# Two-layer graph network with residual and layer norm: successive matmuls of an accumulation alternate between the two PSUM banks of a pair

## The chip, the cores and the metric

The kernel runs on one core of a Trainium2 chip. The metric is the device time of the program in microseconds (us). Before the change it is 2921.07 us, the median of three runs (2920.2 to 2923.01).

## The reference, cut to what matters

```python
def sage_conv(x, src, dst, W_l, b_l, W_r):        # x: 100000 x 256, 25000 edges, dst is sorted
    agg = segment_sum(x[src], dst, 100000)
    deg = segment_sum(ones, dst, 100000)
    return (agg / maximum(deg, 1)[:, None]) @ W_l + b_l + x @ W_r
h = relu(sage_conv(x, src, dst, W1_l, b1, W1_r))
h = relu(sage_conv(h, src, dst, W2_l, b2, W2_r))
out = layernorm(x + h @ W3 + b3)                  # no scale, no shift, eps 1e-5
```

All weights are 256 x 256, and everything is float32.

## The kernel before

**Precision.** Every product is made of three matmuls in fp32r. A float32 operand is split into a high part (ScalarE copies it to fp32r) and a low part (VectorE subtracts the high part from the original), and hi x hi, hi x lo and lo x hi are added up in PSUM. The contraction over 256 features takes K = 2 steps, so one accumulation of a 256 x 256 weight has 6 matmuls.

**PSUM.** There are four tensors `pair[0..3]` of 128 x 2 x 512 floats. Each is two banks: index 0 and 1 of the middle dimension. Together they are the whole PSUM.

**Two kinds of accumulation.** `columns` (line 851) has the weight block as stationary operand and 512 rows of activations as moving operand (128x512 output). Its caller loops over `m` = 0, 1: column block m goes into bank m, so all matmuls of bank 0 come first, then all of bank 1. `by_rows` (line 862) has 128 rows of activations as stationary operand and the weight as moving operand (128x256 output). Its caller loops over `s` = 0 to 3: row blocks 0 and 1 are the two halves of bank 0, blocks 2 and 3 those of bank 1, one block after the other. `turn` (line 845) transposes 128x128 blocks.

**Row stage.** 196 groups g of 512 rows pass through three layers as if there were no edges. The loop body has u = 0 to 3 (g = 4i + u), and its order is written out by hand for each engine, with semaphores between them. TensorE, in the body at line 952: transposes of group g+2 (`turn_rows`), first layer of g+1 (`columns`, 12 matmuls), an edge piece that depends on u, third layer of g-1 (`by_rows`, 24 matmuls, waits for `hlo_ok[1]`, the low part of the second layer's result), second layer of g (`columns`, 12 matmuls). The edge pieces are: u = 0 and u = 1, eight transposes of gathered rows; u = 2, 24 matmuls by rows for source rows; u = 3, 48 matmuls by rows for destination rows.

ScalarE, body at line 522: `high_x(g+2)`, a square root, `high_h` of the first layer of g+1, an edge copy, `normalise(g-2)`, `high_h` of the second layer of g. `high_h` (line 482) is the only consumer in this stage that takes the two banks one at a time:

```python
for k in range(K):
    act.wait_ge(l_ps[n], g * K + k + 1)
    nc.scalar.activation(ps[:, k], ps[:, k], ACT.Relu, ...)   # L486
act.wait_ge(hf_ok[n], (g + 1) * K)
nc.scalar.copy(h_hi[:, h], ps[:, :, :])                       # L488
```

VectorE, body at line 741: `low_x` (L643), `factors` (L698, L700), `low_h` of the first layer (L647), the edge piece (u = 0: L717 and two scans L721; u = 1: L725 and L727), the residual sum (L669, waits for both banks of the third layer), four `bn_stats` (L681), four `bn_aggr` (L692), `low_h` of the second layer (L647). VectorE takes the results of `by_rows` only when both banks are complete (L669, L731, L738).

**Edge stage.** After the rows come 49 steps j of 512 edge slots (line 1010): `turn_edges(j+1)` (16 transposes; waits for `c_mlo_ok`, the low part of the mean of step j), the second layer of j by `columns` with two weights (24 matmuls: 12 for bank 0, then 12 for bank 1), the third layer of j-1 by rows (24 matmuls). ScalarE (line 577) takes `dst_high(j+1)`, `finish_edges(j-3)` (L568), `second(j, 0)` (relu of bank 0, L553), `mean_high(j+1)` (L548), `second(j, 1)`, `second_high(j)` (L557). VectorE (line 817) takes the residual, factors, two scans (L776), `low_dst` (L787), `means` (L781), the statistics, `mean_low` (L791) and `low_second` (L795).

SyncE loads rows and stores results; GpSimd adds b3 to x (L391, waits for L669 of an earlier group) and issues the indirect DMAs. Neither waits for an accumulation of `columns`.

Of the kernel before, what the change touches and what calls it, by code (L numbers as in the profile page):

```python
# [5 lines left out]
P = 128  # L6
S = 4
# [6 lines left out]
def build(nc, x, src, dst, W1_l, b1, W1_r, W2_l, b2, W2_r, W3, b3, out):  # L14
# [12 lines left out]
    N, D = x.shape  # L27
    E = src.shape[0]
    K = D // P
# [11 lines left out]
    X1R, X2R, X3, X1L, X2L = range(5)  # L41

    with ExitStack() as ctx:
        def sb(name, shape, dt=f32):
            return ctx.enter_context(nc.sbuf_tensor(name, shape, dt))

        def pb(name):
            return ctx.enter_context(nc.psum_tensor(name, [P, K, G], f32))

        def sem(name):  # L50
            return ctx.enter_context(nc.semaphore(name))
# [11 lines left out]
        w_hi = sb("w_hi", [P, 5, K, D], f32r)  # L63
        w_lo = sb("w_lo", [P, 5, K, D], f32r)
        xn = sb("xn", [P, U, S, D])
        xb = sb("xb", [P, 2, S, D])
        xt_hi = sb("xt_hi", [P, 2, K, G], f32r)
        xt_lo = sb("xt_lo", [P, 2, K, G], f32r)
        h_full = sb("h_full", [P, 2, K, G])
        h_hi = sb("h_hi", [P, 3, K, G], f32r)  # L70
        h_lo = sb("h_lo", [P, 3, K, G], f32r)
# [3 lines left out]
        xe_hi = sb("xe_hi", [P, 2, K, G], f32r)  # L75
        xe_lo = sb("xe_lo", [P, 2, K, G], f32r)
# [3 lines left out]
        mean_hi = sb("mean_hi", [P, K, G], f32r)  # L80
        mean_lo = sb("mean_lo", [P, K, G], f32r)
# [25 lines left out]
        pair = [pb(f"pair{n}") for n in range(4)]  # L107
# [22 lines left out]
        l_ps = [sem("l1_ps"), sem("l2_ps")]  # L130
        l3_ps = sem("l3_ps")
# [7 lines left out]
        xs_ps, xd_ps, src_ps, dst_ps = sem("xs_ps"), sem("xd_ps"), sem("src_ps"), sem("dst_ps")  # L139
# [12 lines left out]
        c_hs_ps, c_hd_ps, c_l2_ps, c_l3_ps = (sem(n) for n in (  # L152
            "c_hs_ps", "c_hd_ps", "c_l2_ps", "c_l3_ps"))
# [5 lines left out]
        def after(eng, s, value):  # L159

            if not (isinstance(value, int) and value <= 0):
                eng.wait_ge(s, value)
# [681 lines left out]
        def _(pe):  # L844
            def turn(ps, rows_of, k):

                for s in range(S):
                    ins = nc.tensor.transpose(ps[:, k, s * P:(s + 1) * P], rows_of[:, s, k * P:(k + 1) * P], ident[:, :])  # L848
                return ins

            def columns(parts, ps, m):

                first = True
                for w, hi, lo in parts:
                    for k in range(K):
                        for wx, a in ((w_hi, hi), (w_lo, hi), (w_hi, lo)):
                            end = k == K - 1 and a is lo and w == parts[-1][0]
                            ins = nc.tensor.matmul(ps[:, m], wx[:, w, k, m * P:(m + 1) * P], a[:, k], start=first, stop=end)  # L858
                            first = False
                return ins  # L860

            def by_rows(parts, ps, s):

                first = True
                for w, hi, lo in parts:
                    for k in range(K):
                        for a, wx in ((hi, w_hi), (hi, w_lo), (lo, w_hi)):
                            end = k == K - 1 and a is lo and w == parts[-1][0]
                            ins = nc.tensor.matmul(ps[:, s // 2, s % 2 * D:(s % 2 + 1) * D], a[:, k, s * P:(s + 1) * P],  # L869
                                                   wx[:, w, k], start=first, stop=end)  # L870
                            first = False
                return ins

            def turn_rows(i, u, ps):
                pe.wait_ge(x_in[u], 16 * (i + 1))
# [1 line left out]
                    turn(ps, xn[:, u], k).then_inc(xt_ps, 1)  # L877

            def first_layer(b, ps):
                for m in range(K):  # L880
                    columns([(X1R, xt_hi[:, b], xt_lo[:, b])], ps, m).then_inc(l_ps[0], 1)

            def second_layer(h, ps):
                for m in range(K):
                    columns([(X2R, h_hi[:, h], h_lo[:, h])], ps, m).then_inc(l_ps[1], 1)

            def third_layer(g, ps):
                pe.wait_ge(hlo_ok[1], g + 1)
                for s in range(S):
                    ins = by_rows([(X3, h_hi[:, 2], h_lo[:, 2])], ps, s)  # L890
                    if s % 2:
                        ins.then_inc(l3_ps, 1)


            pe.wait_ge(cleared, 3)
# [3 lines left out]
            for c in range(6):  # L899
                ins = nc.tensor.transpose(pair[1][:, c // S, c % S * P:(c % S + 1) * P], e_idx[:, c // 2, c % 2 * P:(c % 2 + 1) * P], ident[:, :])  # L900
            ins.then_inc(turned_pre, 1)
            pe.wait_ge(prep, PREP_ENDS)
            for n in range(2):
                ins = nc.tensor.transpose(pair[3][:, 0, n * P:(n + 1) * P], tr[:, n], ident[:, :])
# [3 lines left out]
            pe.wait_ge(w_ok, 1)  # L908
            pe.wait_ge(xlo_ok, 1)
            first_layer(0, pair[0])  # L910
            pe.wait_ge(prep, PREP_RDEG)
            turn_rows(0, 1, pair[3])
# [3 lines left out]
            def edges(i, u, ps):  # L916
                xs, xd = (xe_hi[:, 0], xe_lo[:, 0]), (xe_hi[:, 1], xe_lo[:, 1])
                if u == 0:
                    pe.wait_ge(xs_in, 16 * S * (i + 1))
                    for k in range(K):  # L920
                        turn(ps, xe[:, 0], k).then_inc(xs_ps, 1)
                if u == 1:
                    pe.wait_ge(xd_in, 16 * S * (i + 1))
                    for k in range(K):
                        turn(ps, xe[:, 1], k).then_inc(xd_ps, 1)
                if u == 2:
                    pe.wait_ge(xs_ok, i + 1)
                    for s in range(S):
                        ins = by_rows([(X1R, *xs)], ps, s)
                        if s % 2:  # L930
                            ins.then_inc(src_ps, 1)
                if u == 3:
                    pe.wait_ge(mlo_ok, i + 1)
                    pe.wait_ge(xd_ok, i + 1)
                    for s in range(S):
                        ins = by_rows([(X1R, *xd), (X1L, mean_hi, mean_lo)], ps, s)
                        if s % 2:
                            ins.then_inc(dst_ps, 1)

            def edges_left(i, u):  # L940

# [32 lines left out]
            def last_layer(g, b, low_ok, y_s, l3):  # L974
                pe.wait_ge(low_ok, g + 1)
                after(pe, y_s, g)
                for s in range(S):
                    ins = by_rows([(X3, h_hi[:, b], h_lo[:, b])], pair[3], s)
                    if s % 2:
                        ins.then_inc(l3, 1)  # L980

            pe.wait_ge(src_ok, NE)
            pe.wait_ge(dst_ok, NE)
# [3 lines left out]
            for m in range(K):  # L987
                first = True
                for w in (X2R, X2L):
                    for k in range(K):  # L990
                        for wx, a in ((w_hi, b1_hi), (w_lo, b1_hi), (w_hi, b1_lo)):
                            ins = nc.tensor.matmul(pair[2][:, 0, 2 * m:2 * m + 2], wx[:, w, k, m * P:(m + 1) * P], a[:, k],
                                                   start=first, stop=w == X2L and k == K - 1 and a is b1_lo)
                            first = False
            ins.then_inc(bias_ps, 1)

            def turn_edges(j, b):
                pe.wait_ge(c_hs_in[b], slot_use(j, b, 16 * S))
                after(pe, c_mlo_ok, j)
                for k in range(K):  # L1000
                    turn(pair[0], xn[:, b], k).then_inc(c_hs_ps, 1)
                pe.wait_ge(c_hd_in[b], slot_use(j, b))
                after(pe, c_hdlo_ok, j)
                for k in range(K):
                    turn(pair[1], xn[:, 2 + b], k).then_inc(c_hd_ps, 1)
# [4 lines left out]
            def step(j, b, left):  # L1010
                if left:
                    turn_edges(j + 1, 1 - b)
                if isinstance(j, int) and j == 0:
                    pe.wait_ge(y_ok, NG)
                pe.wait_ge(c_mlo_ok, j + 1)
                pe.wait_ge(c_hdlo_ok, j + 1)
                after(pe, c_hlo_ok, j)
                for m in range(K):
                    columns([(X2R, xe_hi[:, b], xe_lo[:, b]), (X2L, xt_hi[:, b], xt_lo[:, b])], pair[2], m).then_inc(c_l2_ps, 1)
                if not (isinstance(j, int) and j == 0):  # L1020
                    last_layer(j - 1, 1 - b, c_hlo_ok, c_y_ok, c_l3_ps)
                if not left:
                    last_layer(j, b, c_hlo_ok, c_y_ok, c_l3_ps)
            edge_passes(pe, step)


# [29 lines left out]
```

## Time and profile before

| | |
|---|---|
| Median of three runs | 2921.07 us (2920.2 to 2923.01) |
| The profiled execution, time and span | 2916.1 us, 2914.3 us |
| TensorE matmul, weight load | 97%, 88% of the span |
| VectorE, ScalarE, GpSimd | 78%, 67%, 62% of the span |
| Mean granted TensorE clock | 0.994 |
| Stages by the span's time | preparation 0 to about 60 us, rows to about 2360 us, edges to 2880 us, last stores to the end |

Busy time of a matmul overlaps that of the next one, so it is the distance from start to start that tells what a matmul costs. DMA and POOL figures count issues and packets.

### The profile page before, as it was taken

Reading aid. Unit: us, or ns where it says so; the run is one execution under the profiler, and the core shown is the slowest. Engines: PE = TensorE matmul, PEld = TensorE weight load, DVE = VectorE, ACT = ScalarE, POOL = GpSimd, SP = SyncE. Lnnn points to the kernel's source line nnn. Section 1 sums busy time; section 2 is a strip of 40 time slices with the busy share of each in tenths; the row PEclk is TensorE's granted clock in tenths of the full one; section 3 lists DMA queues with packets and bytes.
Section 4 is the critical chain, followed back from the end, with each engine's and each line's share of the span. In section 5 each row is a group of like instructions: output and inputs, shape, how many; then the busy total and the mean of one; then the engine's idle time right before and its main releaser. Section 6 shows DMA issues by size and latency. Waiting matters only on the chain. (4 is left out here: it accounts for less than half of the span.)

```text
span 2914.3 us, 54614 instructions
## 1 busy us (share of the span) xinstructions
PE 2835.6 (97%) x18457; PEld 2571.9 (88%) x18457; DVE 2282.0 (78%) x4001; ACT 1958.3 (67%) x2992; POOL 1820.8 (62%) x1732
## 2 busy tenths in 40 slices
PE   5999999999999999999999999999999989999996
PEld 4999999999999999999999999999999979988885
DVE  5787777778787878777777878787877769999996
ACT  3676766767676767676676767676767646666554
POOL 5665656656565656565655656565656547777776
PEclk9999999999999999999999999999999989999998
DMA  4444544444454544454544445444445457766664
GB/s 137 150 156 149 166 144 166 156 147 160 144 169 149 164 148 156 150 166 143 166 152 151 159 144 169 149 164 147 157 150 166 137 169 245 250 244 242 236 239 148
DMA packets 253121, 488.25 MB, mean 168 GB/s; under 512 B 37615, under 2 KB 165206, under 8 KB 253090
## 3 DMA queue, kind: packets, MB, share of 16 engines
q1 hardware_dynamic: 202498, 387.58, 39.6%
q0 software_dynamic: 50176, 99.91, 10.6%
q10 hardware_dynamic: 416, 0.40, 0.0%
q8 instruction: 14, 0.23, 0.0%
q14 instruction: 17, 0.14, 0.0%
HBM read 284.67 MB, written 206.22 MB: 168 GB/s over the span
## 5 line engine op out<-in xcount | busy, mean ns | idle before, releaser
L486 ACT ACTIVATE pair<-pair,bias 128x512 f32<-128x512 f32 x784 | 513.8, 660 | 670.9 <-PE pair L858 656.1
L391 POOL TENSOR_TENSOR xb<-xn,b_row 128x1024 f32<-128x1024 f32 x196 | 469.8, 2397 | 548.2 <-DVE y L669 548.1
L647 DVE TENSOR_TENSOR h_lo<-pair,h_hi 128x1024 fp32r<-128x1024 f32 x392 | 476.8, 1216 | 280.0 <-ACT h_hi L488 279.2
L869 PE MATMUL pair<-w_hi,h_hi 128*128 128x256 f32 x1960 | 562.9, 287 | 4.8 <-DVE h_lo L647 3.1
L869 PE MATMUL pair<-w_lo,h_hi 128*128 128x256 f32 x1960 | 555.0, 283 | 0.0
L869 PE MATMUL pair<-w_hi,h_lo 128*128 128x256 f32 x1960 | 555.0, 283 | 0.0
L345 POOL DMA_INDIRECT xe<-in_x_dram,e_stage x392 | 405.9, 1036 | 176.5 <-issue 97.7
L499 ACT ACTIVATE o<-y,nb,rs 128x256 f32<-128x256 f32 x784 | 407.6, 595 | 3.5 <-DVE nb L700 3.5
L488 ACT CAST h_hi<-pair 128x1024 fp32r<-128x1024 f32 x392 | 398.0, 1015 | 12.5
L858 PE MATMUL pair<-xt_hi,w_hi 128*128 128x512 f32 x980 | 400.6, 409 | 4.1 <-DVE run L721 2.1
L858 PE MATMUL pair<-xt_lo,w_hi 128*128 128x512 f32 x980 | 384.5, 392 | 0.0
L858 PE MATMUL pair<-xt_hi,w_lo 128*128 128x512 f32 x980 | 383.0, 391 | 0.0
L869 PEld LDWEIGHTS pair<-w_hi,h_hi 128*128 128x128 f32 x1960 | 375.9, 192 | 7.3 <-DVE h_lo L647 3.5
L669 DVE TENSOR_TENSOR y<-pair,xb 128x1024 f32<-128x1024 f32 x245 | 298.1, 1217 | 105.1 <-PE pair L869 105.1
L869 PEld LDWEIGHTS pair<-w_lo,h_hi 128*128 128x128 f32 x1960 | 376.5, 192 | 1.9
L869 PEld LDWEIGHTS pair<-w_hi,h_lo 128*128 128x128 f32 x1960 | 376.0, 192 | 0.0
L681 DVE BATCH_NORM_STATS2 stats<-y 128x6 f32<-128x256 f32 x980 | 344.0, 413 | 6.8
L848 PE MATMUL pair<-ident,xn 128*128 128x128 f32 x2352 | 301.7, 275 | 26.7 <-DVE xt_lo L791 11.6
L848 PEld LDWEIGHTS pair<-ident,xn 128*128 128x128 f32 x2352 | 271.4, 141 | 57.5 <-issue 17.8
L858 PE MATMUL pair<-h_hi,w_hi 128*128 128x512 f32 x784 | 307.6, 392 | 0.0
L858 PE MATMUL pair<-h_hi,w_lo 128*128 128x512 f32 x784 | 307.4, 392 | 0.0
L858 PE MATMUL pair<-h_lo,w_hi 128*128 128x512 f32 x784 | 306.0, 390 | 0.0
(124 smaller groups left out, 6192.9 us busy)
## 6 DMA issues: line engine op xcount, KB each, us to landing
xn<-in_x_dram SPq DMA_DIRECT2D x196, 512.0 KB, 4.1
out_dram<-o SPq DMA_DIRECT2D x196, 512.0 KB, 3.0
seg<-seg_tab SPq DMA_DIRECT2D x74, 512.0 KB, 5.1
xdb_tab<-xdb SPq DMA_DIRECT2D x49, 512.0 KB, 4.9
h_tab<-src_h SPq DMA_DIRECT2D x49, 512.0 KB
h_tab<-dst_h SPq DMA_DIRECT2D x49, 512.0 KB, 6.2
xn<-h_tab SPq DMA_DIRECT2D x49, 512.0 KB, 5.1
xb<-xdb_tab SPq DMA_DIRECT2D x49, 512.0 KB, 4.0
```

The source lines that it names most:

```text
L345: nc.gpsimd.indirect_dma_start(out=xe[:, kind, s], out_offset=None, in_=x, in_offset=bass.IndirectOffsetOnAxis(ap=e_stage[:, kind, s:s + 1 ...
L391: nc.gpsimd.tensor_tensor(xb[:, b], xn[:, u], b3_row[:, :].unsqueeze(1).to_broadcast([P, S, D]), ALU.add).then_inc(xb_ok, 1)
L486: nc.scalar.activation(ps[:, k], ps[:, k], ACT.Relu, bias=bias[:, n, k:k + 1]).then_inc(hf_ok[n], 1)
L488: nc.scalar.copy(h_hi[:, h], ps[:, :, :]).then_inc(hhi_ok[n], 1)
L499: ins = nc.scalar.activation(o[:, b, s], y[:, b, s], ACT.Identity, bias=nb[:, b, s:s + 1], scale=rs[:, b, s:s + 1])
L647: nc.vector.tensor_tensor(h_lo[:, h], ps[:, :, :], h_hi[:, h].bitcast(f32), ALU.subtract).then_inc(hlo_ok[n], 1)
L669: nc.vector.tensor_tensor(y[:, b].rearrange("p s d -> p (s d)"), ps[:, :, :].rearrange("p k g -> p (k g)"), xb[:, b].rearrange("p s d -> p ...
L681: ins = nc.vector.bn_stats(stats[:, s], y[:, b, s])
L848: ins = nc.tensor.transpose(ps[:, k, s * P:(s + 1) * P], rows_of[:, s, k * P:(k + 1) * P], ident[:, :])
L858: ins = nc.tensor.matmul(ps[:, m], wx[:, w, k, m * P:(m + 1) * P], a[:, k], start=first, stop=end)
L869: ins = nc.tensor.matmul(ps[:, s // 2, s % 2 * D:(s % 2 + 1) * D], a[:, k, s * P:(s + 1) * P], wx[:, w, k], start=first, stop=end)
```

## The change

The loop over `m` moves inside `columns`, and the loop over row blocks inside `by_rows`. Every matmul, with its operands, stays; only their order changes, and the semaphore is raised by the last matmul of each bank. Raises are as many as before.

```diff
-            def columns(parts, ps, m):
+            def columns(parts, ps, done):
                 first = True
                 for w, hi, lo in parts:
                     for k in range(K):
                         for wx, a in ((w_hi, hi), (w_lo, hi), (w_hi, lo)):
                             end = k == K - 1 and a is lo and w == parts[-1][0]
-                            ins = nc.tensor.matmul(ps[:, m], wx[:, w, k, m * P:(m + 1) * P], a[:, k], start=first, stop=end)
+                            for m in range(K):
+                                ins = nc.tensor.matmul(ps[:, m], wx[:, w, k, m * P:(m + 1) * P], a[:, k], start=first, stop=end)
+                                if end:
+                                    ins.then_inc(done, 1)
                             first = False
-                return ins
-            def by_rows(parts, ps, s):
-                first = True
-                for w, hi, lo in parts:
-                    for k in range(K):
-                        for a, wx in ((hi, w_hi), (hi, w_lo), (lo, w_hi)):
-                            end = k == K - 1 and a is lo and w == parts[-1][0]
-                            ins = nc.tensor.matmul(ps[:, s // 2, s % 2 * D:(s % 2 + 1) * D], a[:, k, s * P:(s + 1) * P],
-                                                   wx[:, w, k], start=first, stop=end)
-                            first = False
-                return ins
+            def by_rows(parts, ps, done):
+                for side in range(2):
+                    first = True
+                    for w, hi, lo in parts:
+                        for k in range(K):
+                            for a, wx in ((hi, w_hi), (hi, w_lo), (lo, w_hi)):
+                                end = k == K - 1 and a is lo and w == parts[-1][0]
+                                for bank in range(2):
+                                    s = 2 * bank + side
+                                    ins = nc.tensor.matmul(ps[:, bank, side * D:(side + 1) * D], a[:, k, s * P:(s + 1) * P],
+                                                           wx[:, w, k], start=first, stop=end)
+                                    if end and side:
+                                        ins.then_inc(done, 1)
+                                first = False
             def first_layer(b, ps):
-                for m in range(K):
-                    columns([(X1R, xt_hi[:, b], xt_lo[:, b])], ps, m).then_inc(l_ps[0], 1)
+                columns([(X1R, xt_hi[:, b], xt_lo[:, b])], ps, l_ps[0])
```

`second_layer`, `third_layer`, the edge pieces at u = 2 and u = 3, `last_layer` and the second layer of the edge stage change in the same way. In a first or second layer bank 0 is then complete with the 11th of 12 matmuls where it was with the 6th; in the edge stage with the 23rd of 24 where it was with the 12th. Bank 1 is complete with the last one, as before. ScalarE and VectorE keep their programs.

## Rows read from the trace of the kernel before

**Rows 1.** The page, part 1: busy time of each engine.
```profile
PE 2835.6 (97%) x18457; PEld 2571.9 (88%) x18457; DVE 2282.0 (78%) x4001; ACT 1958.3 (67%) x2992; POOL 1820.8 (62%) x1732
```

**Rows 2.** Windows: stretch, length; busy PE, PEld, DVE, ACT, POOL; clock; DMA share, GB/s.
```profile
500.00:2360.00 1860.00, 1857.27 (x12240) 1691.23 (x12238) 1418.81 (x2510) 1307.00 (x1999) 1121.66 (x1053) 1.00 0.47 154
...
2420.00:2500.00 80.00, 80.00 (x508) 72.31 (x507) 79.26 (x136) 51.35 (x80) 61.89 (x60) 1.00 0.73 249
...
2600.00:2700.00 100.00, 97.08 (x618) 87.05 (x617) 95.61 (x165) 60.85 (x95) 77.13 (x76) 1.00 0.67 240
```

**Rows 3.** Windows of line 858 alone, then line 869 alone: PE and weight load.
```profile
0.00:2915.00 2915.00, 1440.44 (x5880) 1075.66 (x5880) 0.99 0.50 167
...
0.00:2915.00 2915.00, 1176.39 (x9408) 1154.93 (x9408) 0.99 0.50 167
```

**Rows 4.** Timeline of PE, u = 1: start, duration, instruction; third layer, then second layer.
```profile
1003.94 0.28 PE L869 MATMUL pair<-w_hi,h_lo 128*128 128x256 f32 x1
1004.06 0.28 PE L869 MATMUL pair<-w_hi,h_hi 128*128 128x256 f32 x1
...
1006.66 0.39 PE L858 MATMUL pair<-h_lo,w_hi 128*128 128x512 f32 x1
1006.89 0.39 PE L858 MATMUL pair<-h_hi,w_hi 128*128 128x512 f32 x1
...
1008.02 0.39 PE L858 MATMUL pair<-h_lo,w_hi 128*128 128x512 f32 x1
```

**Rows 5.** Timelines of PE and of ACT, u = 0 (last row: u = 1).
```profile
991.41 0.40 PE L858 MATMUL pair<-xt_lo,w_hi 128*128 128x512 f32 x1
...
990.93 0.66 ACT L486 ACTIVATE pair<-pair,bias 128x512 f32<-128x512 f32 x1
991.84 0.66 ACT L486 ACTIVATE pair<-pair,bias 128x512 f32<-128x512 f32 x1 [0.25 <-PE pair L858]
...
1001.58 1.22 ACT L486 ACTIVATE pair<-pair,bias 128x512 f32<-128x512 f32 x2
```

**Rows 6.** Timeline of DVE, u = 3 and u = 0, and the window from 993.58 to 1001.25.
```profile
989.97 1.23 DVE L647 TENSOR_TENSOR h_lo<-pair,h_hi 128x1024 fp32r<-128x1024 f32 x1 [1.35 <-ACT h_hi L488]
...
993.58 1.23 DVE L647 TENSOR_TENSOR h_lo<-pair,h_hi 128x1024 fp32r<-128x1024 f32 x1 [0.97 <-ACT h_hi L488]
...
1001.25 1.19 DVE L647 TENSOR_TENSOR h_lo<-pair,h_hi 128x1024 fp32r<-128x1024 f32 x1
...
993.58:1001.25 7.67, 7.67 (x47) 6.76 (x46) 7.53 (x13) 6.11 (x9) 4.65 (x5) 1.00 0.41 147
```

**Rows 7.** Timeline: third layer's first weight load at u = 1; a stalled weight load, edge stage.
```profile
1002.52 0.19 PEld L869 LDWEIGHTS pair<-w_hi,h_hi 128*128 128x128 f32 x1
...
2579.12 1.00 ACT L548 CAST xt_hi<-pair 128x1024 fp32r<-128x1024 f32 x1
...
2580.16 1.23 DVE L791 TENSOR_TENSOR xt_lo<-pair,xt_hi 128x1024 fp32r<-128x1024 f32 x1 [1.72 <-ACT xt_hi L548]
...
2581.44 0.64 PEld L848 LDWEIGHTS pair<-ident,xn 128*128 128x128 f32 x6 [1.06 <-DVE xt_lo L791]
```

**Rows 8.** Timelines of one edge step: PE, PEld, ACT, DVE.
```profile
2501.39 0.47 PE L858 MATMUL pair<-xe_hi,w_hi 128*128 128x512 f32 x1
...
2506.49 0.39 PE L858 MATMUL pair<-xt_hi,w_lo 128*128 128x512 f32 x1
...
2511.48 0.47 PE L858 MATMUL pair<-xe_hi,w_hi 128*128 128x512 f32 x1
...
2509.72 1.77 PEld L848 LDWEIGHTS pair<-ident,xn 128*128 128x128 f32 x16
...
2506.38 1.01 ACT L548 CAST xt_hi<-pair 128x1024 fp32r<-128x1024 f32 x1 [1.18 <-DVE pair L781]
...
2507.57 1.20 DVE L791 TENSOR_TENSOR xt_lo<-pair,xt_hi 128x1024 fp32r<-128x1024 f32 x1
...
2509.04 1.23 DVE L795 TENSOR_TENSOR h_lo<-pair,h_hi 128x1024 fp32r<-128x1024 f32 x1
```

More of the change, by code:

```diff
@@ L879, in first_layer @@
             def first_layer(b, ps):
-                for m in range(K):
-                    columns([(X1R, xt_hi[:, b], xt_lo[:, b])], ps, m).then_inc(l_ps[0], 1)
+                columns([(X1R, xt_hi[:, b], xt_lo[:, b])], ps, l_ps[0])
             def second_layer(h, ps):
-                for m in range(K):
-                    columns([(X2R, h_hi[:, h], h_lo[:, h])], ps, m).then_inc(l_ps[1], 1)
+                columns([(X2R, h_hi[:, h], h_lo[:, h])], ps, l_ps[1])
             def third_layer(g, ps):
                 pe.wait_ge(hlo_ok[1], g + 1)
[L889 to L892, printed above, removed]
+                by_rows([(X3, h_hi[:, 2], h_lo[:, 2])], ps, l3_ps)
             pe.wait_ge(cleared, 3)
@@ L927, in edges @@
                     pe.wait_ge(xs_ok, i + 1)
[L928 to L931, printed above, removed]
+                    by_rows([(X1R, *xs)], ps, src_ps)
                 if u == 3:
@@ L934, in edges @@
                     pe.wait_ge(xd_ok, i + 1)
[L935 to L938, printed above, removed]
+                    by_rows([(X1R, *xd), (X1L, mean_hi, mean_lo)], ps, dst_ps)
             def edges_left(i, u):
@@ L976, in last_layer @@
                 after(pe, y_s, g)
[L977 to L980, printed above, removed]
+                by_rows([(X3, h_hi[:, b], h_lo[:, b])], pair[3], l3)
             pe.wait_ge(src_ok, NE)
@@ L1017, in step @@
                 after(pe, c_hlo_ok, j)
-                for m in range(K):
-                    columns([(X2R, xe_hi[:, b], xe_lo[:, b]), (X2L, xt_hi[:, b], xt_lo[:, b])], pair[2], m).then_inc(c_l2_ps, 1)
+                columns([(X2R, xe_hi[:, b], xe_lo[:, b]), (X2L, xt_hi[:, b], xt_lo[:, b])], pair[2], c_l2_ps)
                 if not (isinstance(j, int) and j == 0):
```

## The prediction

> **What bounds the kernel now.** I read the page first, then windows by stage, then timelines. By the page TensorE is busy for 97% of the span, well ahead of the others [rows 1]. The windows refine that. In the row stage (500 to 2360 us) PE is busy 1857.27 of 1860 us at the full clock (2.4 GHz), while VectorE and ScalarE have a quarter to a third of their time free: the stage lasts as long as TensorE's own stream. In the edge stage VectorE is nearly as full: 79.26 of 80 us, beside 80.00 of PE. Later there, at 2600 to 2700 us, PE already shows 2.9 us of holes in 100, still at the full clock [rows 2]. So two things can move the time: the distance between matmuls, and new waits of TensorE. The change touches both. It puts each matmul in another bank than its predecessor, and it completes bank 0 later.
>
> **Part 1: the distance between matmuls.** In a third layer the twelfth and thirteenth matmul start 0.12 us apart, and there the output moves from bank 0 to bank 1. In the second layer behind it the sixth and seventh start 0.23 us apart, also at a change of bank, and from the seventh to the twelfth, all in bank 1, it is (1008.02 - 1006.89) / 5 = 0.226 us [rows 4]. At 2.4 GHz 256 columns take 0.107 us and 512 take 0.213 us, so every matmul has some 13 ns on top. But a matmul that changes the bank has the same 13 ns as one that stays in it. If a matmul had to wait for the adder of its own bank, the changes would be shorter; if a change cost something, they would be longer. I take 0 for all 5880 + 9408 = 15288 matmuls [rows 3]. The bounds: the rows have a resolution of 10 ns, and a single change might hide a small effect that a steady alternation shows. 1 ns a matmul is 15 us. Weight loads stay as many and as large; in `by_rows` the two matmuls of hi x hi and hi x lo with the same stationary rows are no longer neighbours, but both are loaded anew already: each line has as many weight loads as matmuls [rows 3]. I cost that at 0, too.
>
> The Trainium skill speaks for more here: Perfetto Trace Analysis, Matmul Optimizations, asks that all PSUM banks be used for instruction-level parallelism, and TensorE: Matmul & The Clock Gate, Back-to-back issue gap, gives N/2.4 + 2.5 ns, by which some 11 ns a matmul are to be had. The rows at the bank change speak against the first as the way to the second; what it would give is a rival below. A rule against this change is in Perfetto Trace Analysis, Optimizing Tensor Performance: groups should rotate through banks so that the evacuation of one overlaps the matmuls of the next. That is the overlap which part 2 prices.
>
> **Part 2: bank 0 is complete later.** Consumers of `by_rows` wait for both banks, and the last matmul is where it was: cost 0, nothing hides it. Only the relus that take one bank at a time are concerned, L486 and L553.
>
> *Row stage.* Take u = 0. The last first-layer matmul starts at 991.41 and ends at 991.81; the relu of bank 1 starts at 991.84, that is 0.03 us behind. The relu of bank 0 had run at 990.93 [rows 5]. After the change bank 0 is complete one matmul before the end: 991.81 - 0.23 = 991.58, relu at 991.61. Two relus back to back take 1.22 us with the second at 0.66, so they start 0.56 us apart [rows 5]: the relu of bank 1 starts at 992.17 instead of 991.84. The delay is 0.56 - 0.23 = 0.33 us, and the copy L488 behind it inherits it, as does L647 on VectorE, which waited 0.97 us for exactly that copy [rows 6].
>
> Who waits for this next? Behind L647 VectorE has the edge copy, two scans, the residual, statistics and at last L647 of the second layer. From 993.58 to 1001.25 it is busy 7.53 of 7.67 us [rows 6], so nothing absorbs the 0.33 us. ScalarE's copy for that last L647 was ready earlier, so this chain alone sets it. It ends at 1001.25 + 1.19 = 1002.44. It releases the third layer of u = 1, whose first weight load starts at 1002.52 [rows 7]. The margin looks like 0.08 us, but a wait has a latency: in the edge stage a weight load that really waited started 0.05 us after VectorE's end (2580.16 + 1.23 = 2581.39, load at 2581.44) [rows 7]. So 0.03 us are free, and the third layer at u = 1 comes 0.33 - 0.03 = 0.30 us late. The rest of TensorE's stream shifts behind it.
>
> At u = 2 and u = 3 the edge pieces put 24 and 48 matmuls ahead of the third layer (2.9 and 5.8 us at 0.12), where at u = 0 and 1 there are eight transposes (0.8 us). VectorE then waits for PE and is back in step, so the 0.30 us comes once per body. At u = 0 the third layer needs the L647 of the u = 3 before. That one ends at 989.97 + 1.23 = 991.20 [rows 6], before the last first-layer matmul starts at 991.41 [rows 5], and eight transposes (0.8 us) still lie between: 1 us of margin, where 0.33 does no harm. I count 48 bodies: **48 x 0.30 = 14.4 us**. Bounds: 0 if ScalarE's delay were absorbed somewhere, and 48 x 0.38 = 18 us if the 0.03 us are no margin and refilling the array costs 0.05.
>
> *Side effects.* GpSimd's L391 and its gathers wait for L669, and SyncE for the results; both come 0.3 us later in a body. GpSimd is busy 1121.66 of 1860 us [rows 2], so I cost it at 0. If that cover were gone, each body would pay those 0.3 us again, 14 us in all.
>
> *Edge stage.* Write C for the start of a step's first matmul, 2501.39. The next step starts at 2511.48: the period is 10.09 us. The 23rd matmul starts at 2506.49, C + 5.10 [rows 8]. After the change it is bank 0's last and ends 0.39 us later, C + 5.49, and the relu of bank 0 starts at C + 5.52. The mean's copy L548 comes directly behind it, 0.6 us later (two L486 of the same size start 0.56 apart [rows 5]): C + 6.12, where it was at 2506.38, C + 4.99. So here the delay is 1.1 us, and L548 is no longer held by VectorE (it waited 1.18 us for L781) but by ScalarE. L791 starts 1.04 us after L548 where it really waits (2579.12 to 2580.16) [rows 7], so at C + 7.16, and ends with 1.20 at C + 8.36; plus 0.05 it releases the next 16 transposes at C + 8.41. Their first weight load stood at 2509.72, C + 8.33 [rows 8]. TensorE gets 0.08 us late. The second relu, L557 and L795 follow: L795 started at C + 7.65 (2509.04), and 1.1 us later it ends at about C + 10.0, just ahead of the next columns at C + 10.1. VectorE has 80 - 79.26 = 0.74 us free in eight periods, 0.09 a step [rows 2], and runs 1.1 us later against TensorE. 47 steps x 0.09 = **4.2 us**. Here the cushion of 1 us between TensorE and the others is used up. Below, 0. Above: the holes that are there, 2.9 us in 100 [rows 2], could double once each disturbance reaches TensorE undamped, 0.5 us a step, 23 us.
>
> **The sum.** 0 + 14.4 + 4.2 = 18.6 us. The profiled execution has 2916.1 us (span 2914.3), so that one would take 2934.7. The median of the runs, 2921.07, lies 5 us above it; I put the same sum on the median: **2939.7 us**, 0.6% slower. No stall is long enough to cost clock: the edge stage with its stalls kept a granted clock of 1.00 [rows 2].
>
> **The rivals.**
> - *Alternation removes the 13 ns (faster).* The place is every matmul, the price 15288 x 13 ns = 199 us, so 2722; with a twelfth of that the sum above is cancelled, so this decides from some 1.2 ns a matmul. For it: the 13 ns exist. Against it: they are there at a change of bank as well. Chance 5%.
> - *The delay is absorbed (no change).* The relus' 0.33 us do not reach L647 at u = 1, or the wait has more room than it seems. Then 2921 to 2926. For it: the margin is read from 10 ns rows. Against it: VectorE's stretch has no gap. Chance 13%.
> - *The edge stage loses its cushion (slower still).* Forecast of the row stage plus 23 us: 2921 + 14 + 23 = 2958. For it: VectorE at 99%. Against it: a late `finish_edges` holds L548 now; after the change L548 is late anyway, and both delays overlap. Chance 17%.
> - *Alternation lengthens the distance* by 1 ns or so, with the stalls: about 2955. Nothing in the rows shows it. Chance 5%.
> - That the change does not do what it says: the order in the code is plain and TensorE executes in order, so I give it nothing.
>
> **How the numbers follow.** The forecast has 60%, and the two slower rivals 22%: slower by over 0.2% (5.8 us, about what a measurement here can tell from no change) 82%. No change 13%, faster 5%. The likeliest case's own range is 2930 to 2946 (row stage 10 to 18, edge stage 0 to 8). The range for 8 in 10 reaches up to the lost cushion and down to the edge of no change: 2924 to 2957.
>
> **What the profile after would show.** In the row stage the starts of matmuls stay 0.12 and 0.226 us apart; relus L486 stand in pairs 0.56 us apart; the wait of L486 for PE grows; a wait of PE or the weight load for L647, about 0.3 us, 48 times, all at line 869 at u = 1; a body takes 0.3 us longer. In the edge stage L548 follows L553 directly, the wait for L781 is gone, and waits of L848 for L791 are frequent and short. A changed distance between matmuls refutes part 1. Waits in the row stage at another u, or of another length than 0.3 us, refute the chain of part 2. A period in the edge stage above 10.3 in undisturbed steps says that the cushion mattered more.

## The result and the profile after

The changed kernel takes 2932.14 us (median of five runs, 2931.54 to 2936.18), the kernel before in the same comparison 2921.07 (five runs, 2918.68 to 2927.29). The ratio is 1.0038 with a 95% interval of 1.0022 to 1.0055: slower by 11 us, somewhere between 6 and 16. Direction and range of the prediction held; the middle was 18.6 us. The profiled execution has a span of 2929.8 us, 15.5 more than the one before.

From the page after, part 1, the slices of granted clock (compare [rows 1]; the page before has two slices at 8, too), and the busiest group of ScalarE, whose wait for PE was 656.1 us before:

```profile
PE 2852.3 (97%) x18457; PEld 2574.4 (88%) x18457; DVE 2285.4 (78%) x4001; ACT 1945.4 (66%) x2992; POOL 1812.3 (62%) x1732
...
PEclk9999999999999999999999999999999989999998
...
L486 ACT ACTIVATE pair<-pair,bias 128x512 f32<-128x512 f32 x784 | 484.2, 656 | 701.2 <-PE pair L859 701.2
```

The same instructions at the same clock. The windows after answer to [rows 2]; columns as there:

```profile
500.00:2360.00 1860.00, 1858.20 (x12167) 1683.40 (x12166) 1415.11 (x2496) 1289.68 (x1988) 1117.42 (x1049) 1.00 0.47 153
...
2420.00:2500.00 80.00, 80.00 (x502) 71.51 (x501) 78.40 (x133) 49.06 (x76) 57.45 (x57) 1.00 0.69 247
...
2600.00:2700.00 100.00, 100.00 (x626) 89.28 (x625) 98.33 (x166) 63.31 (x98) 76.84 (x77) 1.00 0.72 244
```

In 1860 us of the row stage PE gets through 12167 matmuls where it did 12240: 0.6% fewer, with the same busy time, which hides stalls of 0.3 us under the modelled ends. The edge stage shows the contrary: from 2600 to 2700 us PE has no holes now, where it had 2.9 us of them, and does 626 matmuls instead of 618. (At its start, from 2420 to 2500 us, it is still behind, with 502 against 508.) So the loss is in the row stage, and the edge stage gives some back. The first edge step's columns start at 2398.0 us after and 2381.5 before, 16.5 us later; the 47 step periods that follow sum to 485.9 us, before to 488.5. The last period is longer again (10.15 us against 8.86), and TensorE ends 15.6 us later, so in these two profiles the edge stage gives back 0.9 us net.

**Distance between matmuls.** Timeline of PE after, third layer at u = 1, then second layer; a row of x2 is a pair in the two banks:

```profile
1010.14 0.40 PE L874 MATMUL pair<-w_hi,h_hi 128*128 128x256 f32 x2
...
1012.06 0.40 PE L874 MATMUL pair<-w_hi,h_lo 128*128 128x256 f32 x2
...
1013.69 0.62 PE L859 MATMUL pair<-h_hi,w_hi 128*128 128x512 f32 x2
...
1014.59 0.62 PE L859 MATMUL pair<-h_lo,w_hi 128*128 128x512 f32 x2
```

Eight pairs in 1.92 us are 0.120 us a matmul, two pairs in 0.90 us are 0.225: what [rows 4] had. Over all distances in the row stage from 500 to 2360 us the medians are 0.120 and 0.227 us in both traces.

**The chain at u = 0 and its end at u = 1.** Timelines of ACT, DVE and PEld after:

```profile
998.09 1.24 ACT L486 ACTIVATE pair<-pair,bias 128x512 f32<-128x512 f32 x2 [0.22 <-PE pair L859]
1000.40 1.22 DVE L647 TENSOR_TENSOR h_lo<-pair,h_hi 128x1024 fp32r<-128x1024 f32 x1 [0.98 <-ACT h_hi L488]
...
1008.08 1.19 DVE L647 TENSOR_TENSOR h_lo<-pair,h_hi 128x1024 fp32r<-128x1024 f32 x1
...
1009.32 0.30 PEld L874 LDWEIGHTS pair<-w_hi,h_hi 128*128 128x128 f32 x2 [0.29 <-DVE h_lo L647]
```

The two relus stand back to back (before they were 0.91 us apart, [rows 5]), from one L647 to the next it is 7.68 us as it was 7.67 in [rows 6], and the weight load that had 0.08 us to spare in [rows 7] now waits 0.29 us and starts 0.05 behind VectorE's end (1009.27).

**The edge step.** Timelines of PE, ACT and DVE after, answering to [rows 8]:

```profile
2510.84 0.70 PE L859 MATMUL pair<-xe_hi,w_hi 128*128 128x512 f32 x2
...
2521.03 0.70 PE L859 MATMUL pair<-xe_hi,w_hi 128*128 128x512 f32 x2
...
2516.38 0.66 ACT L553 ACTIVATE pair<-pair,bias_c 128x512 f32<-128x512 f32 x1 [2.19 <-PE pair L859]
...
2516.96 1.02 ACT L548 CAST xt_hi<-pair 128x1024 fp32r<-128x1024 f32 x1
...
2518.04 1.21 DVE L791 TENSOR_TENSOR xt_lo<-pair,xt_hi 128x1024 fp32r<-128x1024 f32 x1
```

The period is 10.19 us here and 10.24 in the median, against 10.09 to 10.10. L553 starts 5.54 us into the step, L548 at 6.12, L791 at 7.20; the prediction had 5.52, 6.12 and 7.16. So each undisturbed step is longer, as forecast, and yet the 47 together are shorter. That was the open question. The waits after: the weight load of the row stage, and L568 of ScalarE for its stores (who waited for what: us in total, times, longest):

```profile
PEld pair L874 <- DVE h_lo L647: 17.5, 49, 3.8
ACT o L568 <- DMA out_dram<-o,idx: 2.2, 1, 2.2
```
The same wait of L568 in the waits of before:

```profile
ACT o L568 <- DMA out_dram<-o,idx: 27.2, 18, 3.3
```

L568 had 18 waits for stores, and now has one. Of the 49 waits for L647, 48 come one body (47.68 us) apart and last 0.29 us in the median; the one of 3.8 us is behind the last body, and the kernel before has one of 3.5 us there.

### The profile page after: what moved, and what is told of

Its sections match the earlier page's. It is cut to its first block and busy times, and to the rows that moved or that the text cites. A ratio compares the mean times of both kernels' runs of the same rounds, so it can differ in the third digit from the quotient of the medians.

```text
span 2929.8 us, 54614 instructions
## 1 busy us (share of the span) xinstructions
PE 2852.3 (97%) x18457; PEld 2574.4 (88%) x18457; DVE 2285.4 (78%) x4001; ACT 1945.4 (66%) x2992; POOL 1812.3 (62%) x1732
## 3 DMA queue, kind: packets, MB, share of 16 engines
q0 software_dynamic: 50176, 99.91, 10.6%
## 5 line engine op out<-in xcount | busy, mean ns | idle before, releaser
L647 DVE TENSOR_TENSOR h_lo<-pair,h_hi 128x1024 fp32r<-128x1024 f32 x392 | 478.4, 1220 | 323.5 <-ACT h_hi L488 318.0
L874 PE MATMUL pair<-w_hi,h_hi 128*128 128x256 f32 x1960 | 403.5, 287 | 7.7 <-DVE h_lo L647 3.4
L874 PE MATMUL pair<-w_lo,h_hi 128*128 128x256 f32 x1960 | 394.8, 283 | 0.0
L874 PE MATMUL pair<-w_hi,h_lo 128*128 128x256 f32 x1960 | 394.5, 283 | 0.0
L669 DVE TENSOR_TENSOR y<-pair,xb 128x1024 f32<-128x1024 f32 x245 | 297.9, 1216 | 90.4 <-PE pair L874 90.4
L859 PE MATMUL pair<-xt_hi,w_hi 128*128 128x512 f32 x980 | 321.5, 409 | 4.0 <-DVE run L721 2.5
L874 PEld LDWEIGHTS pair<-w_lo,h_hi 128*128 128x128 f32 x1960 | 305.2, 192 | 0.0
L859 PE MATMUL pair<-xt_hi,w_lo 128*128 128x512 f32 x980 | 304.8, 392 | 0.0
L859 PE MATMUL pair<-xt_lo,w_hi 128*128 128x512 f32 x980 | 303.8, 391 | 0.0
L429 POOL DMA_INDIRECT xn<-h_tab,h_row x196 | 192.7, 983 | 95.5 <-issue 53.6
L356 POOL DMA_INDIRECT slot_tab<-t_stage x196 | 193.8, 989 | 88.8 <-issue 46.7
L437 POOL DMA_INDIRECT out_dram<-o,idx x196 | 202.3, 1032 | 68.3 <-issue 52.4
```

The costliest lines, as they stand in the source:

```text
L437: nc.gpsimd.indirect_dma_start(out=out, out_offset=bass.IndirectOffsetOnAxis(ap=idx[:, 2, j * S + s:j * S + s + 1], axis=0), in_=o[:, b, s ...
L647: nc.vector.tensor_tensor(h_lo[:, h], ps[:, :, :], h_hi[:, h].bitcast(f32), ALU.subtract).then_inc(hlo_ok[n], 1)
L669: nc.vector.tensor_tensor(y[:, b].rearrange("p s d -> p (s d)"), ps[:, :, :].rearrange("p k g -> p (k g)"), xb[:, b].rearrange("p s d -> p ...
L874: ins = nc.tensor.matmul(ps[:, bank, side * D:(side + 1) * D], a[:, k, s * P:(s + 1) * P], wx[:, w, k], start=first, stop=end)
```

## The experiments

**Theory A** says that only `columns` matters, since only its consumers take one bank at a time, and that the loss is one late chain per body. The rivals say that alternation as such costs or gains. Code in the cuts below is shortened where it says `...`. Each comparison has its own runs of the kernel before, with medians from 2921.1 to 2926.0 us, so ratios are compared, not times of different comparisons.

### Column blocks alone (`e1_columns`)

```diff
-for side in range(2): ...            # in by_rows; with `for bank in range(2)` innermost
+for s in range(S):
+    ins = one_row_block(parts, ps, s)     # the old by_rows
+    if s % 2:
+        ins.then_inc(done, 1)
```


> Only the column blocks alternate between the banks; the row blocks go one after the other as before. Theory A (the relu of bank 0 comes late, and only columns has a consumer that takes one bank at a time): all of the loss stays, 11 us (0.4%) over the kernel before, a body of the row stage takes 0.32 us longer than 47.37, and matmuls stay 0.12 and 0.226 us apart. Rival B (alternation itself costs, in proportion to the matmuls: 5880 of 15288 are columns): some 4 us.

Measured 2932.11 us, ratio 1.0020 (1.0010 to 1.0031); body 47.69 us. The profile is that of the full change: edge periods sum to 484.4 us, L647 releases a waiting weight load 49 times. The ratio is lower than the 0.4% expected, which lies outside its interval, and the 6 us that it stands for would fit rival B's 4 us as well; the 24 runs of before in this comparison spread from 2918 to 2935 us with their median at 2926.0. The body decides here, and not the ratio: it has the whole 0.32 us, the 48 waits of 0.3 us are there, and the distances between the 128x512 matmuls have the mean of before, 228.8 ns, where rival B's 4 us would need 0.7 ns more.

### Row blocks alone (`e2_rows`)

```diff
-for m in range(K):                   # innermost in columns
-    ins = nc.tensor.matmul(ps[:, m], ...)
+for m in range(K):                    # outermost; bank_by_bank is the old columns
+    bank_by_bank(parts, ps, m).then_inc(done, 1)
```


> Only the row blocks alternate; the column blocks go bank by bank as before. Theory A: the time of the kernel before, ratio 1.000 within 0.2%, a body of the row stage 47.37 us. Rival B (alternation itself costs): some 7 us more, since 9408 of 15288 matmuls are of this kind. Rival C (alternation gains in by_rows and the late relu hides it): faster than before by some us.

Measured 2923.83 us, ratio 0.9993 (0.9980 to 1.0005); body 47.43 us (47.37 in the profile of before; other kernels with the old order in the row stage have the one or the other, and what makes the 0.06 us is open). Rival B's 7 us more fall by the interval, which reaches from 6 us less to 1.5 more. Rival C's gain falls by the trace: the distance in `by_rows` has a median of 0.120 us here too, and the body is no shorter. Alternation of 9408 matmuls shows no worth in either direction.

### All but the first layer at u = 0 (`e3_u0_old`)

```diff
-first_layer((u + 1) % 2, pair[(u + 1) % 4])
+first_layer((u + 1) % 2, pair[(u + 1) % 4], u in (0,))   # True: bank by bank
```


> The changed kernel, but the first layer that TensorE computes at u = 0, one of eight column layers of a body, goes bank by bank again. Theory A names this one layer as the start of the chain L486, L488, L647 ... L647 that ends in the third layer of u = 1: a body takes 47.37 to 47.40 us again, no wait of line 874 for L647, and the time falls back to within 0.2% of the kernel before, whatever the other seven layers do. Rival D (every late relu costs its share, spread over the body): seven eighths of the 0.32 us stay, 0.28 us a body, about 10 us over before.

Measured 2917.17 us, ratio 0.9966 (0.9954 to 0.9979); body 47.37 us. This is 14.9 us under `e1_columns` in the same comparison, for one of eight column layers of a body. The waits of this kernel keep a single one of the 49:

```profile
PEld pair L885 <- DVE h_lo L647: 3.8, 1, 3.8
```

The chain is where theory A put it; rival D falls. And the kernel is 0.34% faster than before, outside the 0.2% that theory A allowed: it still alternates in the edge stage, which is taken apart below.

### The delay without alternation (`e4_late_relu`)

```diff
-act.wait_ge(l_ps[n], g * K + k + 1)
+act.wait_ge(l_ps[n], g * K + K)
```


> The kernel before, without any alternation, but in the row stage the relu of bank 0 waits until both banks are complete. The relu of bank 1 then starts 0.56 us late instead of 0.33. Theory A (lateness alone makes the loss): the third layer at u = 1 is late by 0.56 - 0.03 = 0.53 us, a body takes 47.9 us, 48 x 0.53 = 25 us over before (0.9%). Rival B (the loss comes from alternation): the time of before, or less than 0.2% over it.

Measured 2950.74 us, ratio 1.0083 (1.0066 to 1.0101), 24.7 us over before; body 47.95 us. Lateness alone makes the loss, and in about the size that the relu's distance gives: the body grows by 0.52 to 0.58 us (against 47.43 or 47.37), where 0.53 was computed.

### One store less in each edge step, before and after (`e5`, `e6`)

```diff
-for s in range(S):            # scatter of results, and 16 * S in the waits on c_out
+for s in range(S - 1):        # and 16 * (S - 1)
```


> The kernel before, with three of the four indirect stores of results in each edge step; a quarter of the rows of the edge nodes keeps its first value. POOL then issues 7 indirect DMAs a step instead of 8, at 1.29 us each: 9.0 us instead of 10.3. Theory E (POOL's issues bound the edge stage before, 8 x 1.29 = 10.3 us a step against 10.09 of TensorE's own): the late steps of 10.5 to 11.4 us go, all are 10.09, the 47 periods sum to about 475 us instead of 489, and the kernel takes 14 us less, about 2907. Rival F (the irregular steps come from DMA traffic or TensorE's waits, not from the number of issues): less than 5 us.

> The changed kernel, with three of the four indirect stores of results in each edge step; a quarter of the rows of the edge nodes keeps its first value. Theory E (POOL bounds the edge stage in both kernels, and hides the 0.13 us that the change adds to TensorE's period there): periods of 10.22 us, sum about 480 us, and the gap to the kernel before with three stores is 15.4 us of the row stage and 47 x 0.13 = 6 us of the edge stage, 21 us, twice the 11 us with four stores. Rival F: the gap stays 11 us.

Why POOL: in the timeline of POOL before, eight issues and their gaps fill a step, with no wait. First and ninth:

```profile
2508.79 0.99 POOL L429 DMA_INDIRECT xn<-h_tab,h_row  x1 [0.30 <-issue]
...
2519.08 0.99 POOL L429 DMA_INDIRECT xn<-h_tab,h_row  x1 [0.30 <-issue]
```

That is 10.29 us a step, more than TensorE's 10.09. Measured with three stores: the old order 2894.74 us, ratio 0.9909 (0.9894 to 0.9923), 47 periods sum to 472.9 us, none above 10.6; the changed kernel 2923.47 us, ratio 1.0004 (0.9994 to 1.0014), sum 484.1 us, median 10.22. The old order gains 27 us where 14 were expected: 15.6 in the periods (against the profile of before), and 7 behind TensorE's end, where fewer stores are left (14.8 us instead of 22.0). I had forgotten that part. The row stage of this profile ends 3.9 us later than in the profile of before, so that the two profiles differ by 18.6 us, and the profile of before lies 5.6 us under its median in this comparison. The gap between the two is 28.7 us, where 21 was expected and 11 is there with four stores. Theory E holds: with POOL relieved, the longer period of the change is paid. A store left out takes its DMA traffic with it, so rival F is not ruled out by these two runs alone; the table below does that. Of the 11.2 us between the sums 6 are the 0.13 us a step, and the rest lies in the first two periods (12.69 and 11.49 us), whose cause is open.

### Alternation in one stage only (`e7`, `e8`)

```diff
+def rows_columns(parts, ps, done):   # bank by bank
...
-columns([(X1R, ...)], ps, l_ps[0])    # e7: first and second layer of the row stage
+rows_columns([(X1R, ...)], ps, l_ps[0])
...
-columns([(X2R, ...), (X2L, ...)], pair[2], c_l2_ps)       # e8: the edge stage
+rows_columns([(X2R, ...), (X2L, ...)], pair[2], c_l2_ps)
```


> Column blocks alternate in the edge stage alone (and row blocks everywhere); in the row stage column blocks go bank by bank. Theory E: the undisturbed period in the edge stage is 10.2 instead of 10.09 us, but POOL needs 10.3 anyway, so the time is that of the kernel before within 0.2%, or up to 4 us less. Rival G (the cushion between TensorE and the others is worth its 0.13 us a step): 6 us more.

> Column blocks alternate in the row stage alone (and row blocks everywhere); in the edge stage column blocks go bank by bank. Theory A with E: a body takes 47.69 us and the time is 15.4 us over before, if the edge stage is untouched; the changed kernel's 11 us say that its edge stage gives 1 to 4 us back. Rival G: less than the changed kernel's 11 us, about 5 to 9.

Edge stage alone: 2915.56 us, ratio 0.9979 (0.9969 to 0.9990), 6 us under before where at most 4 were expected; body 47.37. Row stage alone: 2936.08 us, ratio 1.0048 (1.0034 to 1.0062), 14.4 us over before; body 47.69. The two parts are apart and have opposite signs. Rival G falls.

### The edge stage's late relu without alternation (`e9`)

Over the profiles so far with four stores, the edge stage falls in two classes. Periods are between the first matmuls of the steps. A long issue is a POOL issue over 1.1 us between the first store and the end. The POOL stretch goes from the start of its first store to the end of its last gather, 336 issues in every kernel; the excess is what its long issues take over 0.985 us, the median issue. The last column counts the waits of L568 for stores in the whole run.

| kernel | order in the edge stage | body, us | 47 periods, us | periods over 10.6 | long issues | POOL stretch, us | excess, us | waits of L568 |
|---|---|---|---|---|---|---|---|---|
| before | bank by bank | 47.37 | 488.5 | 15 | 24 | 448.2 | 16.3 | 18 |
| row blocks alone | bank by bank | 47.43 | 497.0 | 20 | 32 | 456.9 | 24.1 | 28 |
| row stage only | bank by bank | 47.69 | 495.1 | 18 | 29 | 453.2 | 20.9 | 21 |
| late relu in the rows | bank by bank | 47.95 | 501.3 | 20 | 37 | 461.7 | 29.0 | 29 |
| after | alternating | 47.68 | 485.9 | 5 | 16 | 442.4 | 10.3 | 1 |
| column blocks alone | alternating | 47.69 | 484.4 | 4 | 14 | 441.2 | 8.5 | 0 |
| first layer of u = 0 old | alternating | 47.37 | 485.4 | 5 | 16 | 442.6 | 10.3 | 0 |
| edge stage only | alternating | 47.37 | 483.8 | 3 | 14 | 441.9 | 9.8 | 0 |

These are one profile each. The profile of before lies 5 us under its kernel's median, those of the other three with the old order 3 to 10 us above theirs, so no profile of one class reaches the other, but how far apart they usually are is not shown.

In the POOL stretch no pause between two issues is longer than 0.35 us, in any of the eight. Without the excess it takes 431.9 to 432.8 us in all of them. So POOL's own issues set this stretch in both orders, and neither late data nor TensorE holds them up, which leaves nothing for rival F. The difference between the orders in it is that of the long issues, before and after: 448.2 - 442.4 = 5.8 us, against 16.3 - 10.3 = 6.0. Behind the last gather the kernels with the old order need 49.6 to 50.7 us to the end and the alternating ones 51.9 to 53.2, which takes part of it back.

```diff
-act.wait_ge(c_l2_ps, j * K + k + 1)
+act.wait_ge(c_l2_ps, j * K + K)
```


> The kernel before, no alternation anywhere, but in the edge stage the relu of bank 0 waits until both banks are complete. This asks why the edge stage is shorter with alternating columns (47 periods sum to 484 to 486 us in four kernels, 489 to 501 in the four with the old order and four stores). Theory H (the late relu holds TensorE to about POOL's 10.3 us a step, so it never runs ahead to where L568 waits for a store): no waits of L568 for the stores, at most 5 periods above 10.6 us, steady periods of about 10.4 us (relu 0.23 us later than in the changed kernel), sum 484 to 490 us, time 2 to 8 us under before. Rival I (alternation of the banks itself makes the stage even): 15 to 20 periods above 10.6 us and 14 to 24 waits of L568 as in the old order, and a time of before or more.

Measured 2923.19 us, ratio 1.0002 (0.9990 to 1.0013); periods 10.39 to 10.47 but for the first, sum 490.5 us, one above 10.6, no waits of L568. The pattern is theory H's: a late relu alone makes the steps even, and rival I falls by it. The POOL stretch is 439.0 us with an excess of 4.9: 25 issues are over 1.1 us, and none reaches 1.6. The gain did not come: the pace is 0.2 us slower than in the alternating kernels, which takes back what the evenness gives. Theory H's time was a miss.

### The mean's product out of POOL's way (`e10`, `e11`)

The long issues were left. In the profile of before the 14 over 1.6 us behind 2440 us all start within 0.04 to 0.23 us after an L781 starts, in the kernel with alternation in the edge stage only all ten within 0.04 to 0.28; no issue that starts ahead of an L781 is longer than 1.03 us. From the first store on, 42 issues of before start while a product runs. The 24 that start up to 0.90 us into it are all the long ones that there are, and they end 0.81 to 0.89 us behind the product's end, wherever they began: it is as if they stood still until the product is through. Those that start later are normal. One of the long ones, with a normal issue before it, timelines of POOL and DVE before:

```profile
2504.02 1.00 POOL L437 DMA_INDIRECT out_dram<-o,idx  x1 [0.30 <-issue]
2505.33 1.87 POOL L437 DMA_INDIRECT out_dram<-o,idx  x1 [0.31 <-issue]
...
2505.12 1.22 DVE L781 TENSOR_TENSOR pair<-run,src_h 128x1024 f32<-128x1024 f32 x1
```

```diff
-nc.vector.tensor_tensor_scan(run[:, k], seg, pair[0][:, k], run[:, k, G-1:G], ...)
+nc.vector.tensor_tensor_scan(pair[0][:, k], seg, pair[0][:, k], run[:, k, G-1:G], ...)
...
-nc.vector.tensor_tensor(pair[0][:, :, :], run[:, :, :], ...)
+nc.vector.tensor_copy(run[:, :, G-1:G], pair[0][:, :, G-1:G])
+nc.vector.tensor_tensor(pair[0][:, :, :], pair[0][:, :, :], ...)
```


> The kernel before, but in the edge stage the scans write into the PSUM pair that they read, the last column is copied to run, and the mean's product L781 reads PSUM and seg instead of run and seg: one operand in SBUF instead of two. In the profiles of before and e7 all 24 POOL issues over 1.6 us in the stage start within 0.04 to 0.28 us behind the start of an L781, and none that starts ahead of one is long. Theory J (L781 with both inputs in SBUF holds up POOL's descriptor writing, and where this falls decides the length of the stage): no issue over 1.6 us after the first steps, 24 fewer long issues, POOL at 1.29 us an issue; the waits of L568 for the stores shrink, and in spite of some 0.2 us more of VectorE a step (10.25 us) the stage gets 3 to 8 us shorter, the kernel 2914 to 2919. Rival K (long issues come from the queue or from DMA traffic): as many long issues as before, time the same or, by VectorE, up to 8 us more. The Trainium skill, SBUF - State Buffer, Who interferes with whom, says that a VectorE instruction with two SBUF inputs contends with GpSimd's reads; that is theory J.

> The same on the kernel with alternating columns in the edge stage alone (e7). Theory J: the long issues go here, too (10 over 1.6 us). The stage is then set by VectorE and TensorE at 10.2 to 10.4 us a step, so against e7 the gain is small: 0 to 4 us less, or up to 5 more if VectorE's copy lies in TensorE's path, since this order has no room between them. Rival K: long issues stay.

On the kernel before: 2914.58 us, ratio 0.9953 (0.9936 to 0.9969). Not one long issue is left, where there were 24; the sum of the periods is 482.5 us, none above 10.6, and the `o` copy (L569 here) waits for a store once, 1.3 us. The kernel gains 10.4 us against the median of this comparison, more than the 3 to 8 expected. Again 42 issues start while a product (L785 in this kernel) runs, and none takes over 1.03 us, where 24 of the 42 were long. One that starts 0.05 us behind the product's start, timelines of POOL and DVE:

```profile
2441.64 0.95 POOL L430 DMA_INDIRECT xn<-h_tab,h_row  x1 [0.30 <-issue]
...
2441.59 1.23 DVE L785 TENSOR_TENSOR pair<-pair,seg 128x1024 f32<-128x1024 f32 x1
```

On the kernel with alternation in the edge stage only: 2917.57 us, ratio 0.9970 (0.9956 to 0.9983), no long issue either, periods 10.34 us in the median, sum 485.5; it was 10.31 on the kernel before. With the long issues gone, alternation buys nothing: the kernel with it is 3 us slower in the same comparison, though the intervals overlap. Theory J holds, K falls. The Trainium skill, SBUF — State Buffer, Who interferes with whom, says that a VectorE instruction with two SBUF inputs contends with a GpSimd instruction that reads SBUF. These runs agree, and put up to 1.1 us on an issue, 17 us of excess from the first store to the end in the profile of before.

Four versions beat the kernel before in their comparisons: the product in PSUM (0.9953), everything alternating but the first layer at u = 0 (0.9966), the product in PSUM with alternation in the edge stage (0.9970), and alternation in the edge stage only (0.9979). The interval of each overlaps or touches those of its neighbours.

## Why the prediction was right in its direction, and 7.5 us too high

**What bounds the kernel.** Right for the row stage. For the edge stage I named VectorE beside TensorE, by busy time [rows 2], and never asked for POOL, whose 77% leave out the 0.30 us between two issues. Eight issues take 10.3 us, more than TensorE's 10.09, and POOL does not pause from its first store to its last gather: this was the bound. It is the step of the prediction that failed.

**Part 1, the distance: 0 forecast, 0 measured.** The reading was that a single change of bank in [rows 4] already shows what steady alternation would. `e2_rows` confirms it for the rows, and the distances after for both kinds.

**Part 2, row stage: 14.4 us forecast, 15 measured.** A body grows from 47.37 to 47.68 us, 0.31 against 0.30, times 48. The comparisons say 14.9 (one layer put back) and 14.4 (row stage only). Against the bodies of 47.43 us it would be 12. The start (first layer at u = 0), the place of the wait (third layer at u = 1) and the size (relu distance less one matmul, less the margin) are each shown by a run. The longer delay in `e4_late_relu` (0.56 us for 0.33) gave 24.7 us where 25 was computed.

**Side effects at 0.** Held in the row stage: GpSimd waits for L669 and follows.

**Part 2, edge stage: +4.2 us forecast, -0.9 net in the profiles (-2.6 in the 47 periods), about -6 in `e7_edge_only`.** The chain inside a step was right, with every start within 0.05 us. The size came in part by luck: 0.09 us a step was taken from VectorE's free time, which no run ties to the period; measured is the weight load of the transposes at C + 8.46 (2519.30) where it stood at C + 8.33, 0.13 us later, and the period grew by as much. But POOL's queue hid it. What turned the sign is the excess of the long issues, 9.8 us in `e7_edge_only` and 10.3 after against 16.3 before, and `e10` and `e11` show that it can be removed. The waits of L568 for stores (27.2 us before) are for stores that this same queue issues. POOL does not pause for them, and that they cost time of their own is not shown. `e9` shows that a late relu alone removes them. Why the old order's steps meet L781 with more issues is not shown either, nor what makes the end behind the last gather 1 to 4 us longer with alternation.

**The rivals.** Removal of the 13 ns (5%) and lengthening (5%) are refuted. Absorption in the row stage (13%) did not occur. The lost cushion (17%) is there, but costs only where POOL is relieved, as in `e6`, and then 6 us in the steady steps and not 23. The sentence against it, that both delays overlap, fits the waits of L568, which went away; it did not name the queue behind them.

## What to carry to other kernels

In this case the distance at a single change of bank in the old trace already told that alternation gains nothing; look there before reordering. If nothing shows there, alternation only makes the earlier bank late, and the price is read at the consumer that takes the banks one at a time: follow its delay until an engine has a gap, and compare with the margin in the wait at the end of the chain. For a queue of DMA issues take the distance from issue to issue times their number, not the busy time, before naming a bound.

## What the runs showed of the hardware

- POOL shows 77% in a stage that it bounds: each indirect issue takes 0.98 us of busy time and 0.30 us before the next.
- A POOL issue of an indirect DMA that starts just behind a VectorE product of two SBUF operands (128x1024, 1.22 us) takes 1.80 to 2.07 us instead of 0.98 (25 of the 25 that start within 0.3 us, before and in `e7`). All 24 of before that start up to 0.90 us into it end 0.81 to 0.89 us behind its end. With one operand in PSUM none is over 1.03 us.
- A wait for DMA landings need not cost what it shows: 27.2 us of L568's waits turned into 2.2, while POOL's 336 issues without a pause took 5.8 us less, all of it in the long ones.
- Matmuls that alternate between two banks start as far apart as those that stay in one: 0.120 us (128x256) and 0.227 us (128x512), medians of the row stage.
